# Attention inside a gated block with experts: other places for the shared units, and another engine that clears the output bank

## The reference, cut to what matters

```python
# x (8,512,256), ctx (8,512,192); 16 heads of 16; 8 experts of hidden 1024; everything float32
def xattn(query, key_value):
    q, k, v = (query @ Wq + bq), (key_value @ Wk + bk), (key_value @ Wv + bv)   # split into heads
    attn = clip(einsum('bhqd,bhkd->bhqk', q, k) * scale, -10000, 10000)
    attn = softmax(attn)                        # uniform if any value is nan
    return einsum('bhqk,bhkd->bqhd', attn, v).reshape(B, Nq, Cq) @ Wo + bo
def ffn(x):
    logits = x @ gate_weight.T
    gates = logits * (logits >= kth_val)        # one threshold over all logits
    return sum over experts e of gates[e] * (gelu(x @ w1[e].T + b1[e]) @ w2[e].T + b2[e])
x = x + tanh(g_xattn) * xattn(layernorm(x), ctx)
x = x + tanh(g_ffn) * ffn(layernorm(x))
```

## Time and profile before

| | |
|---|---|
| median of 3 runs | 1896.85 us |
| the profiled execution's own time | 1896.23 us |
| its span, first to last instruction | 1894.4 us |
| busy: PE (matmuls) / DVE / ACT / POOL | 1862.6 / 1291.1 / 1277.7 / 146.9 us |
| share of the span: PE / DVE / ACT / POOL | 98% / 68% / 67% / 8% |
| mean granted TensorE clock | 0.991 |

### The profile page before, as it was taken

How to read it: one execution, slowest core, us unless ns; L and a number is a source line. 1 busy time by engine, 2 the same in 40 slices (tenths; PEclk the granted TensorE clock), 3 DMA queues, 4 the chain that set the end, 5 groups by cost and what they waited for, 6 DMA issues and landing times.

```text
span 1894.4 us, 25738 instructions
## 1 busy us (share of the span) xinstructions
PE 1862.6 (98%) x8868; PEld 1349.0 (71%) x8868; DVE 1291.1 (68%) x2279; ACT 1277.7 (67%) x2145; POOL 146.9 (8%) x327
## 2 busy tenths in 40 slices
PE   7999999999999999999999999999999999999998
PEld 6844444444478777887888788788878888887886
DVE  6789999999666665656556666755665676556555
ACT  4447778777855556767666676766667676666665
POOL 6201101111135200000000000000000000000000
PEclk9969999999999999999999999999999999999999
DMA  8933333233113254333232333233233423222321
GB/s 284 374 81 84 87 91 88 79 88 110 38 50 129 107 210 151 119 117 110 90 111 89 133 138 124 95 112 112 89 112 129 151 93 117 111 90 89 121 101 58
DMA packets 97245, 220.84 MB, mean 117 GB/s; under 512 B 31314, under 2 KB 49492, under 8 KB 87892
## 3 DMA queue, kind: packets, MB, share of 16 engines
q1 hardware_dynamic: 97108, 219.12, 33.5%
HBM read 178.57 MB, written 40.24 MB: 116 GB/s over the span
## 4 chain that ended last, share of the span: by engine, by line
PE 89%; ACT 3%; DVE 2%; issue 1%; POOL 0%; ACTq 0%; DVEq 0%; POOLq 0%
PE ps_y L2169 32%; PE ps_h L2116 28%; PE ps_t L862 7%; PE ps_o L873 6%; PE ps_h L2089 5%; PE ps_y L2101 4%; PE ps_s L851 2%; PE ps_m L898 2%; PE ps_m L884 1%; ACT w_raw L1170 1%; DVE low L1007 1%; PE ps_m L890 0%; ACT gelu L2366 0%; PE ps_m L919 0%; PE ps_m L905 0%
## 5 line engine op out<-in xcount | busy, mean ns | idle before, releaser
L2469 DVE TENSOR_TENSOR h_lo<-gelu,h_hi 128x512 fp32r<-128x512 f32 x512 | 352.8, 693 | 437.0 <-ACT h_hi L2369 405.7
L2116 PE MATMUL ps_h<-x_hi,w_pair 128*128 128x512 f32 x1568 | 562.3, 392 | 1.8 <-ACT gelu L2366 0.8
L2366 ACT ACTIVATE gelu<-early,b 128x512 f32<-128x512 f32 x336 | 243.2, 724 | 229.5 <-DVE early L2618 220.7
L2116 PEld LDWEIGHTS ps_h<-x_hi,w_pair 128*128 128x128 f32 x1568 | 294.3, 188 | 78.3 <-issue 6.0
L1007 DVE TENSOR_REDUCE low<-ps_s 128x1 f32<-128x512 f32 x512 | 322.1, 681 | 26.1 <-PE ps_s L851 23.1
L2369 ACT ACTIVATE h_hi<-gelu 128x512 fp32r<-128x512 f32 x448 | 283.5, 633 | 41.9 <-ACT gelu L2366 1.1
L2116 PE MATMUL ps_h<-x_lo,w_pair 128*128 128x512 f32 x784 | 309.4, 395 | 0.0
L2618 DVE TENSOR_TENSOR early<-ps_h,copy 128x512 f32<-128x512 f32 x336 | 230.5, 686 | 49.4 <-PE ps_h L2116 49.4
L1170 ACT ACTIVATE probs_T<-ps_t 128x512 f32<-128x512 f32 x384 | 206.4, 594 | 45.5 <-PE ps_t L862 44.6
L851 PE MATMUL ps_s<-k_st,q_st 48*128 48x512 f32 x512 | 205.0, 481 | 3.2 <-SPq L755 2.0
L2169 PE MATMUL ps_y<-h_hi,w_lo 128*128 128x512 f32 x512 | 202.7, 396 | 0.0
(11 more groups left out here) (263 smaller groups left out, 2536.4 us busy)
## 6 DMA issues: line engine op xcount, KB each, us to landing
x_hi<-blocks_scratch SPq DMA_DIRECT2D x28, 1024.0 KB, 5.2
x_lo<-blocks_scratch SPq DMA_DIRECT2D x28, 1024.0 KB, 8.8
x_hi<-blocks_scratch SPq DMA_DIRECT2D x28, 768.0 KB, 6.7
x_lo<-blocks_scratch SPq DMA_DIRECT2D x28, 768.0 KB, 10.2
gate<-gates_scratch SPq DMA_DIRECT2D x64, 256.0 KB, 3.2
q_st<-q_scratch SPq DMA_DIRECT2D x192, 64.0 KB, 2.3
k_st<-k_scratch SPq DMA_DIRECT2D x192, 64.0 KB, 2.3
k_scratch<-k_hl SPq DMA_DIRECT2D x8, 1024.0 KB, 5.6
```

What stands on the lines that cost most here:

```text
L2116: mm = pe.matmul(bank, w[wp], x[xp], start=start and n == 0, stop=n == 2, skip_group_check=not start)
L2366: act.activation(gelu[:, c % GELUS, :], src, ACT.Gelu_apprx_tanh, bias=b1[p][:, j:j + 1]).then_inc(gelu_done, 1)
L2469: dve.tensor_tensor(h_lo[:, j % RING, :], gelu[:, j % GELUS, :], h_hi[:, j % RING, :].bitcast(F32), ALU.subtract).then_inc(h_ready, 1)
```

## The change

The three tables get other entries: the same units, the same ones of them in the same sequence through the bank, but at other steps and places. `HALVES` is emptied, so the output projection's first part is one unit of eight matmuls. ScalarE, behind a wait for the eight constants, clears `ps_o` with a copy of zeros, and VectorE's memset is gone. VectorE's wait for the constants stands in front of its first check.

```diff
--- before.py
+++ after.py
@@ -538,29 +538,29 @@
 
 
 SHARED = {
-    (0, 0, 2): ("low", 0, 1), (0, 1, 2): ("out", -1, 3), (0, 2, 2): ("rows", -1, 0), (0, 2, 3): ("rows", -1, 1),
-    (1, 0, 0): ("y", -1, 0), (1, 1, 1): ("y", -1, 1), (1, 1, 3): ("low", 0, 2), (1, 2, 0): ("out", 0, 0),
-    (1, 3, 0): ("x2T", -1, 0), (2, 0, 2): ("x2T", -1, 1), (2, 1, 0): ("low", 0, 3), (2, 2, 1): ("out", 0, 1),
-    (2, 3, 1): ("xnT", -1, 0), (3, 0, 0): ("xnT", -1, 1), (3, 1, 3): ("low", 1, 0), (3, 2, 1): ("out", 0, 2),
-    (3, 3, 0): ("logits", -1, 0), (3, 3, 3): ("pick", -1, 0),
+    (0, 0, 1): ("low", 0, 1), (0, 1, 1): ("out", -1, 3), (0, 2, 2): ("rows", -1, 0), (0, 3, 1): ("rows", -1, 1),
+    (1, 0, 2): ("y", -1, 0), (1, 1, 2): ("y", -1, 1), (1, 1, 3): ("low", 0, 2), (1, 2, 1): ("out", 0, 0),
+    (1, 3, 1): ("x2T", -1, 0), (2, 0, 1): ("x2T", -1, 1), (2, 1, 0): ("low", 0, 3), (2, 2, 1): ("out", 0, 1),
+    (2, 3, 1): ("xnT", -1, 0), (3, 0, 1): ("xnT", -1, 1), (3, 1, 0): ("low", 1, 0), (3, 1, 2): ("out", 0, 2),
+    (3, 2, 1): ("logits", -1, 0), (3, 3, 1): ("pick", -1, 0),
 }
 
-HALVES = {(0, 3, 2): ("y", -1, 0)}
+HALVES = {}
 
 VECTOR_AT = {
-    (0, 1, 3): [("out", -1, 3)], (0, 2, 1): [("check", 0, 1)], (1, 0, 0): [("y", -1, 0)],
-    (1, 0, 3): [("statistics", -1, 0), ("statistics", -1, 1)], (1, 1, 1): [("check", 0, 2), ("y", -1, 1)],
+    (0, 1, 3): [("out", -1, 3)], (0, 3, 0): [("check", 0, 1)], (1, 0, 2): [("y", -1, 0)],
+    (1, 0, 3): [("statistics", -1, 0), ("statistics", -1, 1)], (1, 1, 1): [("check", 0, 2)], (1, 1, 2): [("y", -1, 1)],
     (1, 1, 3): [("statistics", -1, 2), ("statistics", -1, 3)], (1, 2, 1): [("out", 0, 0)], (1, 3, 3): [("norm", -1, 0)],
-    (2, 0, 1): [("norm", -1, 1)], (2, 0, 2): [("check", 0, 3)], (2, 1, 0): [("norm", -1, 2)], (2, 2, 1): [("out", 0, 1)],
-    (2, 2, 2): [("norm", -1, 3)], (2, 3, 1): [("xnT", -1, 0)], (3, 1, 1): [("xnT", -1, 1)], (3, 2, 2): [("out", 0, 2)],
-    (3, 3, 0): [("check", 1, 0)], (3, 3, 3): [("pick", -1, 0)],
+    (2, 0, 0): [("norm", -1, 1)], (2, 0, 3): [("check", 0, 3)], (2, 1, 1): [("norm", -1, 2)], (2, 1, 3): [("norm", -1, 3)],
+    (2, 2, 1): [("out", 0, 1)], (2, 3, 2): [("xnT", -1, 0)], (3, 0, 2): [("xnT", -1, 1)], (3, 1, 2): [("out", 0, 2)],
+    (3, 3, 1): [("check", 1, 0), ("pick", -1, 0)],
 }
 
 SCALAR_AT = {
-    (0, 0, 3): [("copy", -1, 3), ("low", 0, 1)], (0, 2, 2): [("rows", -1, 0)], (0, 2, 3): [("rows", -1, 1)],
-    (1, 1, 0): [("copy", 0, 0)], (1, 1, 2): [("low", 0, 2)], (1, 3, 2): [("x2T", -1, 0)],
-    (2, 0, 3): [("x2T", -1, 1), ("copy", 0, 1)], (2, 1, 0): [("low", 0, 3)], (2, 3, 1): [("xnT", -1, 0)],
-    (3, 0, 0): [("xnT", -1, 1)], (3, 0, 3): [("copy", 0, 2)], (3, 1, 2): [("low", 1, 0)], (3, 3, 0): [("logits", -1, 0)],
+    (0, 0, 0): [("low", 0, 1)], (0, 0, 2): [("copy", -1, 3)], (0, 2, 1): [("rows", -1, 0)], (0, 3, 3): [("rows", -1, 1)],
+    (1, 0, 3): [("copy", 0, 0)], (1, 1, 3): [("low", 0, 2)], (1, 3, 3): [("x2T", -1, 0)], (2, 0, 1): [("x2T", -1, 1)],
+    (2, 1, 0): [("copy", 0, 1)], (2, 1, 2): [("low", 0, 3)], (2, 3, 0): [("xnT", -1, 0)], (3, 0, 1): [("xnT", -1, 1)],
+    (3, 0, 3): [("copy", 0, 2), ("low", 1, 0)], (3, 2, 3): [("logits", -1, 0)],
 }
 
 V_PLACE = 3
@@ -993,9 +993,6 @@
                 lambda: pe.wait_ge(taken["pick"], BATCH // HELD)]
 
     def vector(dve, first_weights):
-        dve.memset(ps_o[:], 0.0).then_inc(o_zeroed, 1)
-        dve.wait_ge(consts_set, 8)
-
         def lows(b, g, t, i, turn):
             if t == 0 and i == 0:
                 wait(dve, in_psum["low"], group_no(b, g) - 1)
@@ -1008,6 +1005,8 @@
 
         def check_lows(b, g):
 
+            if (b, g) == (0, 0):
+                dve.wait_ge(consts_set, 8)
             dve.wait_ge(low_done, group_no(b, g) * GROUP * TT + GROUP * TT)
             wait(dve, lows_checked, group_no(b, g))
             dve.scalar_tensor_tensor(out=fits[:, 0, :], in0=low[:, g % 2, :], scalar=FITS, in1=fits[:, 0, :],
@@ -1162,6 +1161,9 @@
 
 
     def scalar(act):
+        act.wait_ge(consts_set, 8)
+        act.activation(ps_o[:], zero[:, 0:1].to_broadcast([P, SEQ]), ACT.Copy).then_inc(o_zeroed, 1)
+
         def exps(b, g, k, i, turn):
             n = quad_no(b, g, k)
             if i == 0:
```

## The result

The changed kernel takes 1906.39 us, the median of six runs (1902.65 to 1909.23), against 1896.63 for the kernel before (six runs, 1895.07 to 1897.63): ratio 1.0051, 95% interval 1.0040 to 1.0061. I had forecast 1894.2. The profiled execution took 1909.23, the slowest of the six; its span is 1907.4.

The account below looks back on a forecast made before the run. TensorE's chain was taken as the bound. Terms of -1.7, -0.4, -0.4 and -0.4 gave -2.9, cut by a tenth to -2.6: 1893.6 us profiled, 1894.2 median, own range 1892 to 1896.5, overall 1889.5 to 1899.

Parts of the forecast that it names:

- Part 1: The tables in a full batch: step changes summing to -0.28 us a batch, -1.7 for batches 1 to 6.
- (0,1): Attention step: out unit moves to place 1 and ScalarE's copy ahead of the last exponential; 2.94 to 3.07 us, +0.13.
- Part 4: Last batch's first-expert work: add ends near 505, before the subtraction at about 508, so the logits find their bank: 0.
- rival C: Last batch: GpSimd's add and the first-expert subtraction meet, holding the logits by 2.0 us: 1896.2 us; chance 0.12.
- part 3: The fill: missing memset and wait taken as 0, ScalarE's clear hidden, SyncE's sends and loads not moved.
- Rival B: VectorE's backlog at the batch's end not absorbed, two steps in seven batches losing 7.4 us: 1901.6 us; chance 0.09.
- (2,3): Attention step: 2.89 us by the price list, with its second pair waiting 0.17 for the third reduction of (2,2).
- (3,1): Attention step holding low and out, cut in three: 3.29 us plus 0.10 of waits for the split, 3.39.
- The step prices: TensorE costs per step from timeline spacings, such as 2.89 us with a transpose unit behind place 1, 2.73 without a unit.
- (0,2) to (1,1): Four attention steps, with the whole projection in (1,0) and (1,1): 14.75 to 14.59 us, -0.16.
- the forecast gain of a full batch: Part 1's sum over steps (0,1) to (3,3): -0.28 us; a full batch was to take 50.4.
- The 54.3 us: Time over the attention that ScalarE's exponentials hold TensorE, read from the waits beside VectorE's 14.9 us.

Follow-up runs that it names:

- the kernel with the early check: Changed kernel with only VectorE's check of group (1,0) moved from (3,3,1) to (3,2,0): 1894.31 us, ratio 0.9990 to the kernel before.
- low-last run: Early check at (3,2,0), ScalarE's output-bank copy at (0,0,3), low unit of (3,1) moved behind the values, otherwise the changed kernel: 1894.63 us, ratio 0.9990.
- tables-only run: Changed kernel's tables with the fill of before (VectorE clears the bank and waits for the constants at its start): 1907.11 us, ratio 1.0058.
- late check: Kernel before with only the check of group (1,0) moved from (3,3,0) to (3,3,3): 1910.77 us, ratio 1.0082.
- one input: Changed kernel with the check's two instructions taking one tensor instead of two, at the same place beside the whole add: 1907.36 us, ratio 1.0050.
- check first: Changed kernel with the check of group (1,0) back at (3,3,0), its place in the kernel before: 1908.43 us, ratio 1.0079.

## Why the prediction was wrong

- **What failed** is a term put at nothing without a reason. Part 1 goes from (0,1) to (3,3); neither the step (0,0) nor the move of VectorE's check to (3,3,1) has a place in it, so the check counts as its own time and (0,0) as its old 2.82. In its place the check took 1.34 to 2.00 us in each of seven batches. That cost 9.2 us in (0,0), 2.4 in (0,1) and 0.5 in (0,2), the half clock in them counted in: all of the 12 against the kernel with the early check (1909.23 against 1897.40, profile to profile).
- **I had the mechanism in hand and looked at one place only.** Part 4 and rival C weighed exactly this meeting for the first-expert subtraction of the last batch, where it didn't happen: there the subtraction took 1.23 us behind the add (517.61 + 2.37 = 519.98), as forecast. I never laid the moved checks beside the add. The trace had what it takes: adds starting 0.3 to 0.8 us ahead of a batch, the check ended 1.0 to 1.3 us before them. And part 3 says that "neither queue moves", though the residual's load follows the send of the low unit that was brought forward by most of a step. Part 4 does move the last batch's add 2.2 us earlier, but for the normalised rows, which the low-last run shows not to be what sets it.

```profile
521.56 1.23 DVE L1865 TENSOR_TENSOR w_first_lo<-early,w_first_hi 128x1024 fp32r<-128x1024 f32 x1
```

- **Rival B named the right side and a wrong cause.** VectorE's backlog in (2,2) to (3,1) was absorbed as worked out: (2,3) 3.07 for 3.06, (3,1) 3.41 for 3.39.
- **The step prices held to 0.1, the sum partly by luck.** With the check moved away the time is 1894.31 for a forecast of 1894.2. The errors were 0.1 in (0,1) (the exponentials behind the copy), -0.1 in (0,2) to (1,1) and +0.1 in (2,2) (3.04 for 2.93). But the forecast gain of a full batch was only 0.28, and 0.08 came (50.69 to 50.61, batches 1, 3, 5 and 6). What filled the gap is the 0.5 us in the expert stage that came with the fill and that nothing forecast, and a median that a few microseconds of half clock can move. That agreement does not undo the miss.
- **A reading.** The 54.3 us that the prediction gives for the exponentials is one of two such rows: the one for the tile `w_raw`, also filled by L1170, has 31.9 more. No term used it.

```profile
PEld ps_t L862 <- ACT w_raw L1170: 31.9, 45, 0.9
```

- **The fill** was right where it was priced: the first reductions start at 93.1 instead of 93.0, ScalarE's clear takes 0.60 and nobody waits, and the tables-only run's median shows no difference.
- **Not foreseen: the clock.** In the profile of the changed kernel TensorE's granted clock falls to half twice toward the end of a long (0,0), for 3.4 us in batch 1 and 6.8 in batch 3, where (0,1) took 5.18 and the window's clock is 0.94. Its runs spread from 1902.65 at a mean clock of 0.990 to 1909.23 at 0.984. The runs at 0.990 of the kernel with the early check took 1894.3 to 1896.0. So some 8 us of the loss is there at equal clocks, and what comes on top, 5 us or more in the slowest runs, goes with a lower clock. That TensorE's idle time set off the drops is what the profiles suggest: the five with a wait of over 1 us in five or more batches (the changed kernel, tables only, late check, one input, check first) all have such drops, two to four each, and the others have none in batches 1 to 7. Not every long (0,0) has one: 3.98 in batch 6 has none. It wasn't tested apart from the stall.

## What to carry to other kernels

Before moving a small instruction, look at which long instruction of the other engine it will stand beside, and at what releases that one: GpSimd's add of 2.38 us held up VectorE's comparisons and subtractions from SBUF to SBUF until its end, even those of 16 elements a partition. Where both must be near each other, cut the long one in pieces, or give the short one a form that doesn't wait (here a reduction did not; it did not do the check's work). A forecast by prices per step needs one more pass: every place where a moved piece could meet a neighbour that runs by another clock, here a load's landing.

## What the runs showed of the hardware

- GpSimd's elementwise add on SBUF and VectorE: a comparison with two SBUF inputs, 16 elements wide, waits to the end of the add that it meets (1.85 for 0.16, at most 2.38); a one-input comparison from SBUF to SBUF does too (up to 2.17); a reduction from SBUF doesn't (0.17 at most), nor do instructions that read PSUM beside the same adds: the row minima (0.67 to 0.69), the splits (0.69) and the pick's copies (0.20 to 0.22). The Trainium skill ("SBUF — State Buffer", section "SBUF: two separate sides") has the lock as exclusive and held for the whole instruction, and the two halves of the add bear that out; on the one-input form it fits that "VectorE: DVE Perf Modes" (section "What auto-detection actually checks") lets one SBUF source with an SBUF destination run in a mode with two ports, under a condition on their shapes. The trace doesn't show the mode itself.
- The add itself took 2.36 to 2.41 us whether a check waited for it or not. The exception points the other way round: in the last batch it took 2.72 in the kernel before and 2.69 in the late-check run, where one of VectorE's casts from SBUF to SBUF was still running when it began, and it was 2.37 in the changed kernel, where none was.
- Stalls of about a microsecond on TensorE at the start of a batch (1.05 in batch 1 and 0.92 in batch 3 of the changed kernel) went with drops to the 1.2 GHz clock of 3.4 and 6.8 us; the kernels whose check never waits had none in batches 1 to 7.
